# Two routing chains laid further apart among the steps and entries that carry them

## The reference

```python
# attention
q = ln @ Wq; k, v = split(concat([xn, ln]) @ Wkv)
out = softmax(q k^T / 8) v @ Wout
x = x + layer_norm(out, g_o, b_o)
# experts, on xf = layernorm(x), 1024 tokens
shared = silu(xf @ Ws_up) @ Ws_down
aff = xf @ centroids.T
idx = top_k(aff + expert_biases, 8)
w = sigmoid(aff[idx]); w = w / sum(w)
h = silu(einsum('td,edf->etf', xf, W_up)); y = einsum('etf,efd->etd', h, W_down)
x = x + shared + sum over the chosen experts of w * y
```

## Time and profile before

| | |
|---|---|
| median of three runs | 421.93 us |
| profiled execution | 421.76 us, of which the span is 420.0 us |
| busy PE / PEld / DVE / ACT / POOL | 357.4 / 240.6 / 305.2 / 287.6 / 238.1 us |
| mean granted clock of TensorE | 0.957 of full |
| transposes by DMA | 96, median 3.2 us from issue to landing |

### The profile page before, as it was taken

How to read it: one execution, slowest core, us unless ns; L and a number is a source line. 1 busy time by engine, 2 the same in 40 slices (tenths; PEclk the granted TensorE clock), 3 DMA queues, 4 the chain that set the end, 5 groups by cost and what they waited for, 6 DMA issues and landing times.

```text
span 420.0 us, 7548 instructions
## 1 busy us (share of the span) xinstructions
PE 357.4 (85%) x2369; PEld 240.6 (57%) x2369; DVE 305.2 (73%) x750; ACT 287.6 (68%) x636; POOL 238.1 (57%) x297
## 2 busy tenths in 40 slices
PE   0279687999999999998599799968594998999995
PEld 0157354666666666675356466635363675677773
DVE  2989676787787787788375777746766498887874
ACT  3468776877877777878575979654464677777672
POOL 4236314888888886876696588893676970000000
PEclk9999889999999999999889899999878899999999
DMA  8400211899898989889668477750000000000000
GB/s 246 123 0 1 46 31 25 154 139 180 142 178 123 184 132 148 137 158 134 130 103 154 83 118 126 142 86 0 2 0 1 0 2 1 2 25 1 0 2 25
DMA packets 121127, 34.44 MB, mean 82 GB/s; under 512 B 110976, under 2 KB 120704, under 8 KB 121088
## 3 DMA queue, kind: packets, MB, share of 16 engines
q1 hardware_dynamic: 120656, 32.39, 44.5%
q10 hardware_dynamic: 432, 1.57, 1.2%
HBM read 8.26 MB, written 0.52 MB: 21 GB/s over the span
## 4 chain that ended last, share of the span: by engine, by line
PE 46%; POOL 16%; DVE 13%; DMA 10%; issue 8%; ACT 6%; SPq 1%; POOLq 0%; DVEq 0%; ACTq 0%
DMA pT<-p 8%; PE ps L814 7%; PE ps L752 6%; PE ps L858 5%; POOL p L385 5%; PE ps L754 5%; PE ps L753 5%; POOL p L383 4%; PE ps L990 3%; PE ps L970 3%; DVE v L1233 3%; PE ps L992 3%; PE ps L991 3%; PE ps L895 2%; PE ps L872 2%
## 5 line engine op out<-in xcount | busy, mean ns | idle before, releaser
L385 POOL TENSOR_TENSOR p<-prob,p 128x512 f16<-128x512 f32 x96 | 111.6, 1163 | 7.7
L1190 DVE CUSTOM_DVE_ANT_0 sc<-ps,mask_add 128x512 f32<-128x512 f32 x128 | 83.3, 688 | 34.5 <-PE ps L814 34.2
L547 ACT ACTIVATE prob<-sc,p_bias 128x512 f32<-128x512 f32 x128 | 91.5, 716 | 3.3 <-POOL p L385 1.4
L383 POOL CAST p<-prob 128x512 f16<-128x512 f32 x96 | 58.5, 610 | 58.4 <-ACT prob L547 42.4
L700 ACT ACTIVATE h<-ps 128x512 f32<-128x512 f32 (+1 forms) x66 | 39.4, 596 | 38.8 <-PE ps L754 38.6
L1364 DVE TENSOR_TENSOR h<-h,ps 128x512 f32<-128x512 f32 x64 | 43.8, 684 | 24.9 <-PE ps L970 24.5
L1371 DVE TENSOR_TENSOR h_lo<-h,h_hi 128x512 fp32r<-128x512 f32 (+1 forms) x66 | 49.6, 752 | 3.2 <-ACT h_hi L713 3.0
L752 PE MATMUL ps<-xf_hi,wu_hi 128*128 128x512 f32 x64 | 37.9, 592 | 12.1 <-POOL wu_lo L461 12.1
L858 PE MATMUL ps<-pT,v 128*64 128x256 f16 x768 | 48.1, 275 | 0.0
L713 ACT ACTIVATE h_hi<-h 128x512 fp32r<-128x512 f32 (+1 forms) x66 | 41.3, 626 | 9.8 <-DVE h L1364 9.4
L555 ACT ACTIVATE p_bias<-neg_max,ln_range 128x2 f32<-128x2 f32 x64 | 18.5, 290 | 39.9 <-DVE neg_max L1190 39.9
(11 more groups left out here) (187 smaller groups left out, 761.2 us busy)
## 6 DMA issues: line engine op xcount, KB each, us to landing
wup_s<-in_L_ffn_W_up SPq DMA_DIRECT2D x8, 256.0 KB, 3.5
wdn_s<-in_L_ffn_W_down SPq DMA_DIRECT2D x8, 256.0 KB, 3.7
pT<-p SPq DMA_TRANSPOSE x96, 3.2
wkv_s<-in_L_xattn_Wkv ACTq DMA_DIRECT2D x2, 512.0 KB, 5.8
x_in<-in_x SPq DMA_DIRECT2D x2, 256.0 KB, 7.2
tok<-in_ctx SPq DMA_DIRECT2D x4, 128.0 KB, 8.0
wq_s<-in_L_xattn_Wq ACTq DMA_DIRECT2D x1, 512.0 KB, 8.1
wo_s<-in_L_xattn_Wout SPq DMA_DIRECT2D x1, 512.0 KB, 5.3
```

What stands on the lines that cost most here:

```text
L383: pool.tensor_copy(p16[:, t, 0, :], prob[:, t, :]).then_inc(s_phi, 1)
L385: pool.tensor_tensor(p16[:, t, 1, :], prob[:, t, :], p16[:, t, 0, :], ALU.subtract).then_inc(s_plo, 1)
L547: act.activation(prob[:, t, :], sc[:, t, :], ACT.Exp, bias=p_bias[:, t:t + 1], scale=-1.0, accum_out=p_sum[:, i % 2, t:t + 1]).then_inc(s_ ...
L1190: return dve.tensor_tensor_reduce(sc[:, t, :], ps[:, score_bank(i, t), :], mask_add[:, step(i)[2], :], -SCALE, -LEAST, ALU.add, ALU.min, n ...
```

## The change

Stages keep their order within each chain; most of them move to a later step or entry, and none of their arithmetic changes.

- First chain: `root2(0)` and `refine(0)` go to step 22, `normalise_turned(0)` from the end of 21 to the start of 24, `residual(0)` to the end of 24, the moments to the end of 26, `root2(1)` and `refine(1)` to 27, `expert_input(0)` to the start of 29, `turn_input(0)` to the end of 29, `evac_xf(0)` and `xf_high(0)` to the start of 30. The centroids' transpose goes to iteration 25, its copy to step 26, the first selector quarter to the end of 25. `queries` waits for the centroids' copy at the moved place, and no longer for `xfT`, since the last `queries` is now ahead of `turn_input(0)`.
- Second chain: POOL does `refine(2, 3)` after part 3 (before: 1), `residual(1)` after part 4 (2), `refine(3, 3)` after part 5 (3). So four parts are split before the first refinement. ACT: `normalise_turned(1)` in entry 8 (4), `expert_input(1)` in 17 (14), `evac_xf(1)` in 19 (17), `xf_high(1)` in 20 (18), `sigmoid(1)` in 23 (22). PE: `turn_input(1)` in 18 (16), `affinities(1)` in 21 (20), `turn_gates(1)` in 28 (27). DVE: moments in 12 (9), and each of the five gate stages one entry later.
- POOL splits the shared expert's weights ahead of `xf_low(0)`, no longer behind it.

```diff
@@ POOL
-                if i == FIRST + 5:
+                if i == FIRST + 6:
                     pool.wait_ge(s_std2, 1)
                     refine(0, 1)
-                if i == FIRST + 6:
+                if i == FIRST + 8:
                     residual(0)
-                if i == FIRST + 8:
+                if i == FIRST + 11:
                     pool.wait_ge(s_std2, 2)
                     refine(1, 1)
...
+            split_shared()
             xf_low(0)
             pool.wait_ge(s_k, STEPS)
             pool.wait_ge(s_q, STEPS // 2)
-            split_shared()
...
-                if part == 1:
+                if part == 3:
                     pool.wait_ge(s_var2, 3)
                     refine(2, 3)
-                if part == 2:
+                if part == 4:
                     residual(1)
-                if part == 3:
+                if part == 5:
                     pool.wait_ge(s_var2, 4)
                     refine(3, 3)
@@ ACT, steps
-                if i == FIRST + 6:
+                if i == FIRST + 10:
                     act.wait_ge(s_cent, 1)
...
-                if i == FIRST + 10:
+                if i == FIRST + 14:
                     evac_xf(0)
                     xf_high(0)
-                if i == FIRST + 5:
+                if i == FIRST + 6:
                     root2(0)
                 if i == FIRST + 8:
+                    normalise_turned(0)
+                if i == FIRST + 11:
                     root2(1)
-                if i == FIRST + 9:
+                if i == FIRST + 13:
                     expert_input(0)
...
-                if i == FIRST + 5:
-                    normalise_turned(0)
-                if i in (FIRST + 7, FIRST + 12):
+                if i in (FIRST + 9, FIRST + 12):
                     fill_selector((i - FIRST) // 12)
@@ ACT, entries
-                if n == 4:
+                if n == 8:
                     normalise_turned(1)
-                if n == 8:
+                if n == 11:
                     fill_selector(3)
-                if n == 14:
+                if n == 17:
                     expert_input(1)
-                if n == 17:
+                if n == 19:
                     evac_xf(1)
-                if n == 18:
+                if n == 20:
                     xf_high(1)
-                if n == 22:
+                if n == 23:
                     sigmoid(1)
@@ PE
-                if 2 * j - 2 == FIRST + 6:
+                if 2 * j - 2 == FIRST + 10:
                     pe.wait_ge(s_centT, 1)
-                if 2 * j - 2 == FIRST + 10:
-                    pe.wait_ge(s_xfT, 1)
...
-                if i == FIRST + 5:
+                if i == FIRST + 9:
...
-                if i == FIRST + 9:
-                    pe.wait_ge(s_qlo, i // 2 + 2)
+                if i == FIRST + 13:
+                    pe.wait_ge(s_qlo, STEPS // 2)
                     turn_input(0)
                 if i == FIRST + 14:
-                    pe.wait_ge(s_qlo, STEPS // 2)
                     affinities(0)
...
-                if n == 16:
+                if n == 18:
                     turn_input(1)
-                if n == 20:
+                if n == 21:
                     affinities(1)
-                if n == 27:
+                if n == 28:
                     turn_gates(1)
@@ DVE
-                if i == FIRST + 7:
+                if i == FIRST + 10:
                     dve.wait_ge(s_added, 1)
                     moments(x1_of(0), 4)
...
-                if n == 9:
+                if n == 12:
                     dve.wait_ge(s_added, 2)
...
-                if n == 21:
+                if n == 22:
                     bias_affinity(1)
-                if n == 22:
+                if n == 23:
                     find(1)
-                if n == 24:
+                if n == 25:
                     gates(1)
-                if n == 25:
+                if n == 26:
                     gate_parts(1)
-                if n == 28:
+                if n == 29:
                     take_gates(1)
```

## The result

The changed kernel took 399.52 us (median of four runs, 398.04 to 401.55) against 421.5, a ratio of 0.9469 with a 95% interval of 0.9397 to 0.954. The forecast was 399.6. The profiled execution took 398.04 us, 1.5 less than the median, with a span of 396.3, so 23.7 us of span are to be accounted for. First the head of its page and the chain of work that ended last, which answer to the earlier trace rows: PE's share of the chain rose from 46 to 57%, POOL's fell from 16 to 7%.

What follows compares the result with a forecast made beforehand. PE was taken as the spine, losing 15.7 us in iterations 21 to 26 and 15.5 in ten expert entries to waits and a lowered clock. 421.76 - 10.7 (first chain) - 11.5 (second chain) = 399.6 us, range 393 to 412.

Steps and rivals of the forecast that it cites:

- ACT's two waits go: First chain: ACT's waits of 5.38 and 4.18 us ahead of `normalise_turned(0)` and `expert_input(0)` vanish, 0.9 and 2.1 us spare.
- fourth rival: Steps 24 and 29: POOL lags over a step, ACT waits as before, only the second gain comes; 410 us, chance 0.07.
- What stays of the first chain's loss: Iterations 21 to 26: 5.0 of 15.7 us lost remain (2.8 + 0.9 + 0.4 + 0.9), so 10.7 gained.
- third rival: Attention steps: late DMA transposes and POOL's three stages delay ACT's exponentials, halving the first gain; 405 us, chance 0.11.
- small form: Third rival in iteration 22 only: a weight load ahead of DMA transposes delays POOL's splits; moving it saves 0.5 to 1.5 us.
- Both long waits for weights go: Expert entries 4 and 12: PE's waits of 4.80 and 5.90 us for low weight parts vanish.
- The shared expert's weights ahead of `xf_low(0)` cost nothing: Ahead of the first `up`: splitting these weights first costs nothing, since `up` needs both in whatever order.
- The new wait at `turn_input(1)`: Second chain: one entry less behind `expert_input(1)` makes PE wait 0.7 us (0 to 1.7).
- The 3.3 us for DVE beside POOL: Expert entries: DVE's moments no longer fit beside the matmuls, and POOL's deadlines are tight; together 3.3 us (0 to 12).
- the idle 9.71 us are filled: POOL ahead of `refine(2)`: part 3 ends near 296.1, DVE's guess comes at 296.70, so POOL hardly waits.
- second rival: Expert entries: DVE shuts POOL out, a weight part takes 6.6 us and PE waits; 411 us, chance 0.17.
- fifth rival: Expert entries: brief PE waits hold its clock at 1.2 GHz, 3.1 instead of 1.61 us per entry; 435 us, chance 0.05.

Runs made afterwards that it cites:

- norm_same_step: Changed kernel with `normalise_turned(0)` put back to the end of step 22, where POOL refines, instead of the start of step 24; 406.72 us, ratio 0.9607.
- later_halves: Changed kernel with DVE's moments of entries 0 and 12 each split over two entries, and `turn_input(1)` and all behind it one entry later; 400.11 us.
- late_loads: Changed kernel with the last two parts of the experts' weights loaded at steps 26 and 29 instead of 20 and 23; 401.04 us, ratio 0.949.
- refine_early: Changed kernel with POOL's `refine(2)` put back after part 1 instead of part 3; 406.16 us, ratio 0.96.
- gates_alone: Changed kernel in which POOL holds part 2 until the first half's gates are made; 402.27 us, ratio 0.9512.
- the repeat: The changed kernel itself, unaltered, timed again beside other kernels; 400.37 us, ratio 0.9466 to the kernel before.

## Why the prediction was right, step by step

- **ACT's two waits go** (so not the fourth rival, 410). Shown for both by the trace, and for the first by `norm_same_step`: that one stage put back costs 6 to 7 us. The margin at step 24 came out at 0.8 us.
- **What stays of the first chain's loss.** Forecast 5.0 of 15.7, so a gain of 10.7. In the profile 1.3 stays in iterations 21 to 26 and 2.6 appears in 27 to 30, a gain of 11.8. Over the eleven profiles that have the whole first chain spread out, iterations 21 to 30 took 65.2 to 68.2 us, 66.9 on average, against 77.8 before: 10.9. The size is right, the terms less so. A pair of iterations took 12.54 us undisturbed; 22 and 23 took 13.8 in the profile and 27 and 28 took 14.7, so 1.3 and 2.1 us were lost where the forecast had 1.4 (first `root2`) and 2.3 (moments and second `root2`). But in `later_halves` 22 and 23 took 13.0: with the transpose in time that `root2` cost 0.5, and the rest of the 1.3 followed the transpose, whose lateness the forecast put at nothing.
- **POOL and DMA hold the steps** (third rival, 405): taken at zero, the nearer end. Iteration 22 varies from 6.6 to 9.8 us between these profiles, so its small form is real, 0 to 3 us. ACT's exponentials wait for POOL's splits there by up to 1.0 us, and POOL for a DMA transpose by 2.7 to 4.1 us; in the kernel before it had waited 3.63 at the same place, so the change did not make it late. How late that transpose is decides how long iteration 22 takes, as far as the profiles show. Which transfer makes it late was not found; `late_loads` acquits the experts' weights at step 20. The small late arrays, queued at step 18, were not tried.
- **Both long waits for weights go.** Shown by entries 4 to 13 at pitch and by `refine_early`. PE waited for none of the parts 1 to 5 that stand ahead of or between the refinements, and `sigmoid(1)` found its input with 0.3 us to spare, where the forecast had none. That is partly luck. POOL's parts 4 to 7 took 5.0 to 5.4 us and not the 4.61 of the forecast, so `xf_low(1)` ended 35.7 us behind the start of entry 4 instead of 33.4; ACT came to `sigmoid(1)` at 35.9 instead of 33.1, because the entries behind 13 had fallen back too. The shared expert's weights ahead of `xf_low(0)` cost nothing, as forecast: PE waited 1.91 us ahead of the first `up`, 1.96 before.
- **The new wait at `turn_input(1)`.** Forecast 0.7, measured 0.60.
- **The 3.3 us for DVE beside POOL.** The size was close, 1.7 + 1.6 in the account, and half of the place was not: the forecast looked for it in the moments, where 1.20 us are, and missed the gates' chain ahead of the entries. POOL's old pause covered that chain; filling the pause is what the change did. The step "the idle 9.71 us are filled" was costed by POOL's own times alone and left out who had profited from POOL's silence.
- **POOL as the bound** (second rival, 411) did not come: parts 6 and 7 took (322.46 - 312.38) / 2 = 5.0 us each, not 6.6, and PE waited for neither. The Trainium skill (SBUF — State Buffer, section "SBUF: two separate sides") has the loser of the shared port pair blocked for the whole of the other's instruction. The 128x4 operation of 1.11 us instead of 0.17 in `gates_alone` agrees with that: it began inside a POOL subtraction of 1.27 us and ended 0.02 us behind it. The throughput that the forecast worked out from full exclusion, 6.6 us a part, did not come; why the two streams held each other up for less was not tested.
- **Slower, by a clock granted at 1.2 GHz through the entries** (fifth rival): excluded, the ten entries ran at 1.00.
- **The sum.** The second chain gained 15.5 - 2.2 - 1.7 = 11.6 us in the profile, against 11.5. That forecast and median agree to 0.1 us is luck: terms were off by more than that and made up for each other, and the repeat's median is 400.37.

## What to carry to other kernels

A stage that needs another engine's queued work should stand a whole period behind it when that engine lags by less than a period; the margin to check is the lag in the trace, and it may be under a microsecond. Work that can start at once belongs ahead of a small job that waits for others in the same queue. Before filling an engine's idle time, list what runs on the other engines in that pause: here a 2.6 us chain took 4.5 to 5.5.

## What the runs showed of the hardware that was not expected

The clock behind the same waits differs between executions of one program. In the changed kernel's profile the stretch behind the last step ran at full clock; in its repeat the same stretch, with the same waits of 1.3, 2.0 and 1.0 us or less, ran near 0.55:

```profile
267.50:273.50 6.00, 5.00 (x43) 3.33 (x43) 1.28 (x8) 4.00 (x5) 5.76 (x7) 1.00 0.01 1
```

```profile
269.30:275.30 6.00, 5.15 (x22) 3.23 (x24) 0.56 (x5) 4.12 (x5) 5.76 (x8) 0.55 0.14 26
```

Iteration 31 to entry 4 took 32.7 us in the first and 36.1 in the second; as a whole the two executions took 398.04 and 403.23 us. Not all of it is the clock: DVE's chain of the gates, beside POOL's splits, took 4.45 and 5.4 us. Why the clock fell in one and not in the other stays open. An effect of 1 to 2 us in such a kernel needs more than one profile.
